# Two-layer mixture-of-experts and attention kernel: the routing chain of the expert passes laid out over other slots

## The chip, the cores and the metric

One core of a Trainium2 chip runs the whole program in one launch. The metric is the device time of one execution in microseconds, the median of several runs.

## The reference

The input x is 4 x 1024 tokens of 128 numbers, float32. Six blocks are added to it in turn, each fed by a layer normalisation of x where the code says so. Four of them are expert blocks, and only these are touched:

```python
x = x + 0.5 * _L0_ffn_ref(_layernorm(x), ...)   # ffn0a
x = x + _L0_attn_ref(_layernorm(x), ...)
x = x + 0.5 * _L0_ffn_ref(_layernorm(x), ...)   # ffn0b
x = x + 0.5 * _L1_ffn_ref(_layernorm(x), ...)   # ffn1a
x = x + _L1_attn_ref(_layernorm(x), ...)
x = x + 0.5 * _L1_ffn_ref(_layernorm(x), ...)   # ffn1b
```

A layer-0 expert block has 16 experts of 64 hidden numbers in 4 groups, and a shared one. The router's sigmoid scores plus a bias pick the best 2 groups by their best expert, then the best 4 experts of these; the sigmoid scores are the weights. A layer-1 block has 8 experts of 256 hidden numbers; the best 2 logits are taken, and their softmax over these two are the weights (the kernel writes it as 0.5 + 0.5 tanh of half the difference from their mean sum). Both compute silu(x W1) * (x W3) for every expert, times its weight, and project back to 128 numbers.

## The kernel before, in words

All experts are computed for all tokens, and the weight of an expert that was not picked is zero. `phase_moe` (called four times from `build`) does one expert pass. It goes over the 4096 tokens in 8 groups of 512, and within a group over chunks of 128 hidden numbers: NC is 9 in layer 0 and 16 in layer 1. Every engine runs the same two loops, written out when the program is built, `for h in range(g0 - 2, end)` over groups and `for c in range(NC)` over chunks. One turn of the inner loop is called a slot here. Each engine executes its own list strictly in order and waits on semaphores.

One chunk passes five engines' hands. To keep float32 accuracy each operand is a sum of a high and a low part in the rounded format fp32r, so each product is three matmuls of 512 columns:

- TensorE, `up_and_gate` (L319, L322): three matmuls for gate, three for up, into one of three PSUM banks each.
- ScalarE, `silu` (L401): silu of the gate bank. Then, in the same slot, `high` of the chunk before (L406): the high part of the hidden product.
- VectorE, `scale` (L553): times the expert weights, a row copied over all lanes (the tile `share`); `hide` (L563): times up. In layer 0 the ninth chunk is the shared expert and has no scale.
- GpSimd, `low` (L438): hidden product minus its high part.
- TensorE, `project` (L331 to L333): three matmuls, two slots later (LAG = 2), which wait for low.

Beside the chunks of group h run the preparation steps of the next groups and the last steps of the one before. The dict `slot` says in which slot each stands, and `chain` calls it there, after the chunk's own work on that engine. Steps named in `early` are done for group h + 2, the others for h + 1; yout, yturn and y (the output's evacuation, transposition and addition to x) are for h - 1. The steps in their order:

- stats, aggr (VectorE, L459, L467 to L471): mean and variance; rstd (GpSimd, `invert`, L432 and L434): a power and a product; norm (ScalarE, L371): x normalised, four tiles of 128 x 128 in one go.
- turn (TensorE, L292): four transposes into the PSUM bank `misc`; xh (ScalarE, L377) and xl (VectorE, L475): its high and low part.
- logit (TensorE, L298 to L300), lout (ScalarE, L381), lturn (TensorE, L305): router logits, tokens on lanes.
- r1 to r4 (VectorE, L495 to L540, with ScalarE's tanh at L386 or L391): a chain of small steps of which each waits for the one before (`step`): scores, the 8 largest (L488), marks by match_replace of four tiles (L511, L532), the penalty of groups not kept (L513), the combine weights `comb` (L540). ROUTE is the count of these steps.
- cturn (TensorE, L311): comb transposed; ScalarE copies it to `combt` (L395); SyncE writes it to memory (L266) and copies it back over the lanes as `share` (L273), 16 copies in layer 0 and 8 in layer 1.

All transposes, the logits and y share the one bank `misc`, so their order on TensorE is fixed, and turn waits for comb_t, yturn (L348) for a step of the next group's routing. Memsets of the tile `unread` (L78) stand between some of the small VectorE steps.

In ffn0b and ffn1a the weights of the next phase are loaded in pieces and split (`ahead`, class SplitAhead: L1116 on SyncE, L1124 on ScalarE, L1129 on GpSimd), two pieces a group, in slots 1 and NC // 2 by `piece_at`.

Of the kernel before, what the change touches and what calls it, by code (L numbers as in the profile page):

```python
# [9 lines left out]
ALU = mybir.AluOpType  # L10
# [154 lines left out]
def phase_moe(nc, k, tag, layer, turn_no, ahead=None, out=None):  # L165
# [17 lines left out]
    if first:  # L183
        slot = dict(stats=7, aggr=7, rstd=8, norm=8, turn=0, xh=0, xl=0, logit=2, lout=2, lturn=3,
                    r1=3, r2=4, r3=5, r4=5, cturn=6, yout=2, yturn=4, y=4)
    else:
        slot = dict(stats=13, aggr=13, rstd=14, norm=14, turn=1, xh=1, xl=1, logit=3, lout=3, lturn=5,
                    r1=5, r2=7, r3=9, r4=10, cturn=11, yout=2, yturn=7, y=8)
    early = ("stats", "aggr", "rstd", "norm")
# [18 lines left out]
    def piece_at(g, c):  # L208
        n = 2 * (g - g0 - 1) + (0 if c == 1 else 1)
        return n if ahead is not None and g > g0 and c in (1, NC // 2) and n < ahead.count else None  # L210

    with ExitStack() as ctx:
# [74 lines left out]
        def _(pe):  # L287
# [20 lines left out]
            def cturn(g):  # L308
                pe.wait_ge(route, (g + 1) * ROUTE)
                for t in range(TG):  # L310
                    mm = pe.transpose(misc[0:NE, t * P:(t + 1) * P], comb[:, t, :], k.ident)  # L311
                mm.then_inc(comb_turned, 1)
# [54 lines left out]
        def _(act):  # L367
            def norm(g):
                act.wait_ge(rstd_done, 2 * g + 2)
                for t in range(TG):  # L370
# [42 lines left out]
            for h in range(g0 - 2, end):  # L413
                for c in range(NC):
# [8 lines left out]
                    chain(h, c, (("norm", norm), ("xh", xh), ("lout", lout), ("r1", r1), ("r2", r2), ("cturn", cturn)))  # L423
# [30 lines left out]
        def _(dve):  # L454
# [49 lines left out]

            def r2(g):
                if first:
                    step(top(gext, top_sb), g)
                    step(dve.memset(top_sb[:, :, 2:8], PAD), g)
                    pause(dve, k)
                    for t in range(TG):  # L510
                        ins = dve.match_replace(gmark[:, t, :], top_sb[:, t, :], gext[:, t, :], TAKEN)  # L511
                    step(ins, g)
                    step(dve.tensor_scalar(pen[:].rearrange("p (e t) -> p e t", t=TG),  # L513
                                           gmark[:, :, 0:5].rearrange("p t e -> p e t"), TAKEN, OUT, ALU.not_equal,
                                           ALU.mult), g)
# [5 lines left out]
            def r3(g):  # L521
                if first:
                    wide = pen[:, 0:4 * TG].rearrange("p (e t) -> p t e", t=TG).unsqueeze(3).broadcast_to([P, TG, 4, 4])
# [4 lines left out]
                else:  # L528
                    step(dve.memset(top_sb[:, :, 2:8], PAD), g)
                pause(dve, k)  # L530
                for t in range(TG):
# [1107 lines left out]
```

## Time and profile before

| | us |
|---|---|
| median of 3 runs | 2052.0 (2049.13 to 2074.68) |
| the profiled execution | 2051.49 |
| its span, first to last instruction | 2049.7 |
| mean granted clock of TensorE | 0.924 of full |
| TensorE matmuls busy | 1723.2 (84%) |
| VectorE busy | 1351.5 (66%) |
| ScalarE busy | 1004.0 (49%) |
| GpSimd busy | 736.8 (36%) |

The profile is of one execution, and its instruction records give start and length of each. PE is TensorE's matmuls, PEld its weight loads, DVE VectorE, ACT ScalarE, POOL GpSimd, SPq SyncE's queue. Busy matmuls overlap in the records: they are pipelined. From the first gate matmul of one group to that of the next, the expert passes take the time that the first section of rows below divides by seven. The first gate matmul of ffn0a starts at 34.11 us, that of ffn0b at 912.28, of ffn1a at 1163.58 and of ffn1b at 1715.79.

### The profile page before, as it was taken

How to read it: one execution, taken by the hardware profiler on the slowest of the kernel's cores; microseconds unless marked ns; L12 is line 12 of the kernel's file. 1: busy time of each engine (PE TensorE's matmuls, PEld its weight loads, DVE VectorE, ACT ScalarE, POOL GpSimd, SP SyncE). 2: the span in 40 equal slices, each digit the busy share in tenths (PEclk: the TensorE clock that was granted, in tenths of full speed). 3: DMA queues.
4: the chain of work that ended last, by engine and by line, in shares of the span. 5: the costliest groups of instructions: out<-in, count | busy, mean ns of one | idle time of the engine just before them, and what ended most of it. 6: DMA issues, size and time to landing. Idle time of an engine off the chain costs nothing. (4 is left out here: it accounts for less than half of the span.)

```text
span 2049.7 us, 26334 instructions
## 1 busy us (share of the span) xinstructions
PE 1723.2 (84%) x8440; PEld 1206.2 (59%) x8440; DVE 1351.5 (66%) x4086; ACT 1004.0 (49%) x1687; POOL 736.8 (36%) x693
## 2 busy tenths in 40 slices
PE   3888869899899899968888699989967775989998
PEld 2666645545555555436666477767755664767776
DVE  4676658778778778536656466666667765666665
ACT  3555415555555565644554355455532223555554
POOL 3444411311312211114544355555520102555555
PEclk9999959999999999979888899999988897999999
DMA  4222211111110110003232211211100001121111
GB/s 130 84 78 69 64 28 30 18 24 28 18 34 18 21 31 18 10 25 103 78 104 74 95 42 42 75 50 42 42 1 0 0 0 42 51 84 47 47 52 52
DMA packets 58086, 94.98 MB, mean 46 GB/s; under 512 B 9297, under 2 KB 16850, under 8 KB 57954
## 3 DMA queue, kind: packets, MB, share of 16 engines
q1 hardware_dynamic: 55842, 91.08, 15.9%
q10 hardware_dynamic: 2112, 2.30, 0.4%
q8 instruction: 64, 1.05, 0.2%
q14 instruction: 68, 0.56, 0.1%
HBM read 76.76 MB, written 2.88 MB: 39 GB/s over the span
## 5 line engine op out<-in xcount | busy, mean ns | idle before, releaser
L909 ACT ACTIVATE att_probs<-banks 128x1024 f32<-128x1024 f32 (+3 forms) x384 | 306.1, 812 | 194.1 <-PE banks L820 192.0
L401 ACT ACTIVATE banks<-banks 128x512 f32<-128x512 f32 x384 | 223.3, 582 | 246.3 <-PE banks L319 239.9
L1034 DVE CUSTOM_DVE_ANT_0 banks<-banks,att_mask 128x128 f32<-128x128 f32 (+3 forms) x512 | 234.4, 525 | 70.6 <-PE banks L801 70.1
L801 PE MATMUL banks<-arena 128*128 128x512 f32 (+3 forms) x768 | 249.1, 406 | 27.9 <-DMA arena<-att_parts 15.3
L949 POOL TENSOR_SCALAR_AFFINE_SELECT att_probs<-att_probs 128x512 f32<-128x512 f32 x128 | 81.6, 637 | 419.7 <-ACT att_probs L909 419.7
L801 PEld LDWEIGHTS banks<-arena 128*128 128x128 f32 x768 | 132.7, 197 | 150.5 <-issue 90.8
L438 POOL TENSOR_TENSOR ffn1a_hid_l<-ffn1a_hid,ffn1a_hid_h 128x512 fp32r<-128x512 f32 x128 | 165.6, 1294 | 153.0 <-ACT ffn1a_hid_h L406 153.0
L438 POOL TENSOR_TENSOR ffn1b_hid_l<-ffn1b_hid,ffn1b_hid_h 128x512 fp32r<-128x512 f32 x128 | 165.3, 1292 | 152.1 <-ACT ffn1b_hid_h L406 152.1
L820 PE MATMUL banks<-arena 128*128 128x512 f32 (+3 forms) x768 | 204.4, 351 | 0.5 <-ACT att_probs L909 0.4
L1036 DVE TENSOR_REDUCE att_mx<-banks 128x1 f32<-128x512 f32 x256 | 162.2, 684 | 32.0 <-PE banks L801 31.8
L839 PE MATMUL banks<-att_probs,att_v_aug 128*32 128x512 f32 (+3 forms) x1536 | 166.4, 505 | 0.6 <-POOL att_probs L949 0.5
L553 DVE TENSOR_TENSOR ffn1a_scl<-banks,ffn1a_share 128x512 f32<-128x512 f32 x128 | 88.4, 691 | 103.5 <-ACT banks L401 92.8
L553 DVE TENSOR_TENSOR ffn1b_scl<-banks,ffn1b_share 128x512 f32<-128x512 f32 x128 | 88.4, 691 | 103.1 <-ACT banks L401 92.5
L820 PEld LDWEIGHTS banks<-arena 128*128 128x128 f32 x768 | 137.3, 190 | 26.0 <-ACT att_probs L909 11.3
L438 POOL TENSOR_TENSOR ffn0b_hid_l<-ffn0b_hid,ffn0b_hid_h 128x512 fp32r<-128x512 f32 x72 | 92.4, 1284 | 116.3 <-ACT ffn0b_hid_h L406 116.3
L438 POOL TENSOR_TENSOR ffn0a_hid_l<-ffn0a_hid,ffn0a_hid_h 128x512 fp32r<-128x512 f32 x72 | 92.5, 1286 | 112.5 <-ACT ffn0a_hid_h L406 112.4
L319 PE MATMUL banks<-ffn1a_xh,arena 128*128 128x512 f32 x256 | 106.7, 417 | 0.0
L319 PE MATMUL banks<-ffn1b_xh,arena 128*128 128x512 f32 x256 | 106.6, 416 | 0.0
L322 PE MATMUL banks<-ffn1a_xh,arena 128*128 128x512 f32 x256 | 103.5, 404 | 0.0
L322 PE MATMUL banks<-ffn1b_xh,arena 128*128 128x512 f32 x256 | 103.3, 404 | 0.0
L563 DVE TENSOR_TENSOR ffn1b_hid<-ffn1b_scl,banks 128x512 f32<-128x512 f32 x128 | 88.0, 687 | 4.4
L563 DVE TENSOR_TENSOR ffn1a_hid<-ffn1a_scl,banks 128x512 f32<-128x512 f32 x128 | 88.0, 687 | 4.4
(390 smaller groups left out, 3890.8 us busy)
## 6 DMA issues: line engine op xcount, KB each, us to landing
ffn0a_share<-weight_rows SPq DMA_DIRECT2D x128, 128.0 KB, 3.0
ffn0b_share<-weight_rows SPq DMA_DIRECT2D x128, 128.0 KB, 3.0
ffn1a_share<-weight_rows SPq DMA_DIRECT2D x64, 256.0 KB, 4.3
ffn1b_share<-weight_rows SPq DMA_DIRECT2D x64, 256.0 KB, 4.5
arena<-att_parts SPq DMA_DIRECT2D x16, 384.0 KB
arena<-att_parts SPq DMA_DIRECT2D x128, 48.0 KB
w_raw<-in_ffn_w_dram SPq DMA_DIRECT2D x12, 256.0 KB, 3.2
out_dram<-x SPq DMA_DIRECT2D x8, 256.0 KB, 2.3
```

The costliest lines, as they stand in the source:

```text
L319: mm = pe.matmul(gate_ps[:, num % NB, :], w[:, ws], xx[:, g % 2, :], start=m == 0, stop=m == 2)
L322: mm = pe.matmul(up_ps[:, num % NB, :], w[:, ws], xx[:, g % 2, :], start=m == 0, stop=m == 2)
L401: act.activation(gate if c < NSCALED else sil[:], gate, ACT.Silu).then_inc(silu_done, 1)
L438: pool.tensor_tensor(hid_l[:, num % NH, :], hid[:, num % NH, :], hid_h[:, num % NH, :].bitcast(F32), ALU.subtract).then_inc(low_cut, 1)
L553: dve.tensor_tensor(scl[:, num % 2, :], gate_ps[:, num % NB, :], share[:, c // PER, :], ALU.mult)\
L563: dve.tensor_tensor(hid[:, num % NH, :], scl[:, num % 2, :] if c < NSCALED else sil[:], up_ps[:, num % NB, :], ALU.mult).then_inc(hidden, 1)
L801: mm = pe.matmul(bank[:, at:at + width], q_st[:, n % 3, t * P:(t + 1) * P], k_pad[:, n % 2, j, c * G:c * G + width], start=True, stop=True ...
L820: mm = pe.matmul(score_ps[:, pair, h, 0:c], k_pad[:, n % 2, 2 * pair + h, kb * P:(kb + 1) * P], q_st[:, n % 3, (qg + 1) * G - c:(qg + 1) * ...
L839: mm = pe.matmul(o_ps[32 * j:32 * j + 32, G - c:G], v_aug[:, b % 2, kb, at:at + 32], probs[:, unit % NPROB, j, 0:c], start=kb == 0, stop=k ...
L909: act.activation(probs[:, unit % NPROB, 2 * pair:2 * pair + 2, 0:c], score_ps[:, pair, :, 0:c], ACT.Exp, scale=SCALE).then_inc(exped, 1)
L1034: ins = dve.tensor_tensor_reduce(now, now, mask[:, G - width:G], 1.0, -3e38, ALU.add, ALU.max, best)
L1036: ins = dve.tensor_reduce(best, now, AX.X, ALU.max)
```

## The change

The same work is done with the same instructions. The dict `slot` is new in both layers; norm is cut into two halves of two tiles each (norm and norm2) that stand in slots of their own; the marking by match_replace is one function `taken`, and the routing chain has five parts instead of four. In layer 0 the whole path up to xl is done for group h + 2 (early), with turn, xh and xl in slot 8. The transposition of comb has a further wait, for the addition of y of the group two before (y_added). The pieces of weights loaded ahead are split in slots 3 and 6 (layer 0) or 5 and 10 (layer 1).

```diff
--- before.py
+++ after.py
@@ -181,12 +181,14 @@
     ROUTE = 12 if first else 8
 
     if first:
-        slot = dict(stats=7, aggr=7, rstd=8, norm=8, turn=0, xh=0, xl=0, logit=2, lout=2, lturn=3,
-                    r1=3, r2=4, r3=5, r4=5, cturn=6, yout=2, yturn=4, y=4)
+        slot = dict(stats=0, aggr=1, rstd=1, norm=3, norm2=4, turn=8, xh=8, xl=8, logit=1, lout=1, lturn=2, r1=2, r2=2,
+                    r3=3, r4=4, r5=5, cturn=7, yout=2, yturn=5, y=6)
+        early = ("stats", "aggr", "rstd", "norm", "norm2", "turn", "xh", "xl")
     else:
-        slot = dict(stats=13, aggr=13, rstd=14, norm=14, turn=1, xh=1, xl=1, logit=3, lout=3, lturn=5,
-                    r1=5, r2=7, r3=9, r4=10, cturn=11, yout=2, yturn=7, y=8)
-    early = ("stats", "aggr", "rstd", "norm")
+        slot = dict(stats=11, aggr=12, rstd=12, norm=14, norm2=15, turn=1, xh=1, xl=1, logit=3, lout=3, lturn=4, r1=4,
+                    r2=5, r3=7, r4=8, r5=8, cturn=10, yout=2, yturn=6, y=7)
+        early = ("stats", "aggr", "rstd", "norm", "norm2")
+    PIECES = (3, 6) if first else (5, 10)
 
     def rows(g):
         return slice((g - g0) * G, (g - g0 + 1) * G)
@@ -206,8 +208,8 @@
                 f(g)
 
     def piece_at(g, c):
-        n = 2 * (g - g0 - 1) + (0 if c == 1 else 1)
-        return n if ahead is not None and g > g0 and c in (1, NC // 2) and n < ahead.count else None
+        n = 2 * (g - g0 - 1) + (0 if c == PIECES[0] else 1)
+        return n if ahead is not None and g > g0 and c in PIECES and n < ahead.count else None
 
     with ExitStack() as ctx:
         def sem(name):
@@ -307,6 +309,7 @@
 
             def cturn(g):
                 pe.wait_ge(route, (g + 1) * ROUTE)
+                at_least(pe, y_added, g - 1)
                 for t in range(TG):
                     mm = pe.transpose(misc[0:NE, t * P:(t + 1) * P], comb[:, t, :], k.ident)
                 mm.then_inc(comb_turned, 1)
@@ -367,7 +370,12 @@
         def _(act):
             def norm(g):
                 act.wait_ge(rstd_done, 2 * g + 2)
-                for t in range(TG):
+                for t in range(TG // 2):
+                    act.activation(xn[:, t, :], k.x[:, tile_of(g, t)], ACT.Identity, bias=nshift[:, t:t + 1],
+                                   scale=rstd[:, t:t + 1])
+
+            def norm2(g):
+                for t in range(TG // 2, TG):
                     ins = act.activation(xn[:, t, :], k.x[:, tile_of(g, t)], ACT.Identity, bias=nshift[:, t:t + 1],
                                          scale=rstd[:, t:t + 1])
                 ins.then_inc(norm_done, 1)
@@ -420,7 +428,7 @@
                             high(h * NC + c - 1)
                         if piece_at(h, c) is not None:
                             ahead.high(act, piece_at(h, c))
-                    chain(h, c, (("norm", norm), ("xh", xh), ("lout", lout), ("r1", r1), ("r2", r2), ("cturn", cturn)))
+                    chain(h, c, (("norm", norm), ("norm2", norm2), ("xh", xh), ("lout", lout), ("r1", r1), ("r2", r2), ("cturn", cturn)))
             high(end * NC - 1)
             yout(end - 1)
 
@@ -502,23 +510,32 @@
                     step(dve.tensor_copy(ext[:, :, 0:NE], misc3[:, :, 0:NE]), g)
                     step(top(ext, top_sb), g)
 
+            def taken(rest, dst):
+                pause(dve, k)
+                for t in range(TG):
+                    ins = dve.match_replace(dst[:, t, :], top_sb[:, t, :], rest[:, t, :], TAKEN)
+                return ins
+
             def r2(g):
                 if first:
                     step(top(gext, top_sb), g)
                     step(dve.memset(top_sb[:, :, 2:8], PAD), g)
-                    pause(dve, k)
-                    for t in range(TG):
-                        ins = dve.match_replace(gmark[:, t, :], top_sb[:, t, :], gext[:, t, :], TAKEN)
-                    step(ins, g)
+                else:
+                    step(dve.tensor_tensor(hs[:], top_sb[:, :, 0:1], top_sb[:, :, 1:2], ALU.add), g)
+                    step(dve.scalar_tensor_tensor(df[:], hs[:].broadcast_to([P, TG, E1]), -0.5, ext[:, :, 0:NE],
+                                                  ALU.mult, ALU.add), g)
+
+            def r3(g):
+                if first:
+                    step(taken(gext, gmark), g)
                     step(dve.tensor_scalar(pen[:].rearrange("p (e t) -> p e t", t=TG),
                                            gmark[:, :, 0:5].rearrange("p t e -> p e t"), TAKEN, OUT, ALU.not_equal,
                                            ALU.mult), g)
                 else:
-                    step(dve.tensor_tensor(hs[:], top_sb[:, :, 0:1], top_sb[:, :, 1:2], ALU.add), g)
-                    step(dve.scalar_tensor_tensor(df[:], hs[:].broadcast_to([P, TG, E1]), -0.5, ext[:, :, 0:NE],
-                                                  ALU.mult, ALU.add), g)
-
-            def r3(g):
+                    step(dve.memset(top_sb[:, :, 2:8], PAD), g)
+                    step(taken(ext, mark), g)
+
+            def r4(g):
                 if first:
                     wide = pen[:, 0:4 * TG].rearrange("p (e t) -> p t e", t=TG).unsqueeze(3).broadcast_to([P, TG, 4, 4])
                     ext4 = ext[:, :, 0:NE].rearrange("p t (g e) -> p t g e", e=4)
@@ -526,16 +543,12 @@
                     step(top(ext, top_sb), g)
                     step(dve.memset(top_sb[:, :, 4:8], PAD), g)
                 else:
-                    step(dve.memset(top_sb[:, :, 2:8], PAD), g)
-                pause(dve, k)
-                for t in range(TG):
-                    ins = dve.match_replace(mark[:, t, :], top_sb[:, t, :], ext[:, t, :], TAKEN)
-                step(ins, g)
-                if not first:
                     dve.wait_ge(tanh_done, g + 1)
                     step(dve.tensor_scalar(sig[:], th[:], 0.5, 0.5, ALU.mult, ALU.add), g)
 
-            def r4(g):
+            def r5(g):
+                if first:
+                    step(taken(ext, mark), g)
                 at_least(dve, comb_turned, g)
                 step(dve.scalar_tensor_tensor(comb[:], mark[:, :, 0:NE], TAKEN, sig[:], ALU.is_equal, ALU.mult), g)
                 assert count[0] == ROUTE, count[0]
@@ -574,7 +587,7 @@
                             scale(h, c)
                         hide(h, c)
                     chain(h, c, (("stats", stats), ("aggr", aggr), ("xl", xl), ("r1", r1), ("r2", r2), ("r3", r3),
-                                 ("r4", r4)))
+                                 ("r4", r4), ("r5", r5)))
             add(end - 1)
 
 
```

## Rows read from the trace of the kernel before

**Rows 1.** Windows, seven groups each: PE, PEld, DVE, ACT, POOL, clock, DMA, GB/s.

```profile
34.11:226.91 192.80, 157.69 (x692) 120.35 (x690) 131.50 (x459) 100.75 (x189) 86.84 (x75) 0.97 0.25 79
912.28:1123.05 210.77, 179.89 (x692) 136.17 (x690) 127.20 (x459) 106.72 (x201) 100.71 (x87) 0.83 0.29 89
1163.58:1457.72 294.14, 271.33 (x1133) 207.25 (x1132) 187.86 (x451) 153.19 (x289) 153.70 (x127) 0.94 0.18 57
1715.79:2005.58 289.79, 267.72 (x1132) 204.04 (x1131) 187.43 (x451) 151.86 (x286) 150.31 (x124) 0.96 0.20 62
```

**Rows 2.** Waits in ffn0a, ffn0b, ffn1a, ffn1a: total, times, longest (us).

```profile
PE banks L292 <- ACT ffn0a_xn L371: 14.0, 7, 2.1
...
PE banks L311 <- DVE ffn0b_comb L540: 13.0, 7, 1.9
...
PE banks L331 <- POOL ffn1a_hid_l L438: 21.7, 9, 3.3
...
ACT ffn1a_th L391 <- DVE ffn1a_df L518: 11.5, 7, 1.7
```

**Rows 3.** Timeline of ffn0b, TensorE's matmuls: start us, us, engine, line.

```profile
1046.64 0.39 PE L333 MATMUL banks<-ffn0b_hid_l,wdh 128*128 128x512 f32 x1
1046.87 0.60 PE L348 MATMUL banks<-pack,ffn0b_y_t 128*128 128x128 f32 x4
...
1047.54 0.39 PE L319 MATMUL banks<-ffn0b_xl,wgh 128*128 128x512 f32 x1
...
1055.80 0.63 PE L319 MATMUL banks<-ffn0b_xl,wgh 128*128 128x512 f32 x1
1056.22 0.63 PE L319 MATMUL banks<-ffn0b_xh,wgl 128*128 128x512 f32 x1
```

**Rows 4.** Timeline of ffn1a, one chunk from scale to low.

```profile
1391.54 0.69 DVE L553 TENSOR_TENSOR ffn1a_scl<-banks,ffn1a_share 128x512 f32<-128x512 f32 x1 [0.66 <-ACT banks L401]
1392.27 0.69 DVE L563 TENSOR_TENSOR ffn1a_hid<-ffn1a_scl,banks 128x512 f32<-128x512 f32 x1
...
1393.54 0.58 ACT L401 ACTIVATE banks<-banks 128x512 f32<-128x512 f32 x1 [1.50 <-PE banks L319]
1394.04 0.62 ACT L406 ACTIVATE ffn1a_hid_h<-ffn1a_hid 128x512 fp32r<-128x512 f32 x1
...
1394.74 1.30 POOL L438 TENSOR_TENSOR ffn1a_hid_l<-ffn1a_hid,ffn1a_hid_h 128x512 fp32r<-128x512 f32 x1 [1.33 <-ACT ffn1a_hid_h L406]
```

**Rows 5.** Timeline of ffn1a, the norm path of one group.

```profile
1412.84 0.16 DVE L471 TENSOR_SCALAR ffn1a_veps<-ffn1a_mv 128x4 f32<-128x4 f32 x1
...
1414.12 1.00 POOL L432 TENSOR_TENSOR ffn1a_rstd<-ffn1a_veps,neghalf 128x4 f32<-128x4 f32 x1
...
1415.44 1.65 ACT L371 ACTIVATE ffn1a_xn<-x,ffn1a_nshift,ffn1a_rstd 128x128 f32<-128x128 f32 x4 [2.65 <-POOL ffn1a_nshift L434]
```

**Rows 6.** Timeline: routing of ffn0b; steps beside low in ffn1a, ffn0a.

```profile
1052.33 0.22 DVE L525 TENSOR_TENSOR ffn0b_ext<-ffn0b_ext,ffn0b_pen 128x64 f32<-128x64 f32 x1
...
1053.21 0.09 DVE L532 MATCH_VALUE_LOAD ffn0b_mark<-ffn0b_top,ffn0b_ext 128x8 f32 x1
...
1053.94 0.55 DVE L540 SCALAR_TENSOR_TENSOR ffn0b_comb<-ffn0b_mark,ffn0b_sig 128x64 f32<-128x64 f32 x1
...
1397.55 0.56 DVE L517 TENSOR_TENSOR ffn1a_hs<-ffn1a_top 128x4 f32<-128x4 f32 x1
...
1396.80 1.29 POOL L438 TENSOR_TENSOR ffn1a_hid_l<-ffn1a_hid,ffn1a_hid_h 128x512 fp32r<-128x512 f32 x1 [0.76 <-ACT ffn1a_hid_h L406]
...
172.59 1.28 DVE L470 TENSOR_SCALAR ffn0a_nmean<-ffn0a_mv 128x4 f32<-128x4 f32 x1
```

**Rows 7.** Timeline of ffn0a, the first weights from ScalarE to the first scale.

```profile
34.57 0.59 ACT L395 ACTIVATE ffn0a_combt<-banks 16x512 f32<-16x512 f32 x1 [5.23 <-PE banks L311]
...
36.79 5.63 SPq L273 DMA_DIRECT2D ffn0a_share<-weight_rows  x9
...
40.32 0.69 DVE L553 TENSOR_TENSOR ffn0a_scl<-banks,ffn0a_share 128x512 f32<-128x512 f32 x1 [5.27 <-DMA ffn0a_share<-weight_rows]
```

More of the change, by code:

```diff
@@ L508, in r2 @@
                     step(dve.memset(top_sb[:, :, 2:8], PAD), g)
-                    pause(dve, k)
-                    for t in range(TG):
-                        ins = dve.match_replace(gmark[:, t, :], top_sb[:, t, :], gext[:, t, :], TAKEN)
-                    step(ins, g)
-                    step(dve.tensor_scalar(pen[:].rearrange("p (e t) -> p e t", t=TG),
-                                           gmark[:, :, 0:5].rearrange("p t e -> p e t"), TAKEN, OUT, ALU.not_equal,
-                                           ALU.mult), g)
                 else:
@@ L521, in r3 @@
             def r3(g):
+                if first:
+                    step(taken(gext, gmark), g)
+                    step(dve.tensor_scalar(pen[:].rearrange("p (e t) -> p e t", t=TG),
+                                           gmark[:, :, 0:5].rearrange("p t e -> p e t"), TAKEN, OUT, ALU.not_equal,
+                                           ALU.mult), g)
+                else:
+                    step(dve.memset(top_sb[:, :, 2:8], PAD), g)
+                    step(taken(ext, mark), g)
+            def r4(g):
                 if first:
```

## Prediction, made before the changed kernel ran

> **What bounds the kernel now.** I read the four expert passes alone: the change touches nothing else. A pass is 8 groups; I call one turn of the inner loop over c a slot (9 in the ffn0 passes, 16 in ffn1). The table by windows, from the first gate matmul of group 1 to that of group 8, gives seven whole groups of each pass: 192.80, 210.77, 294.14 and 289.79 us, so 27.5, 30.1, 42.0 and 41.4 us a group [rows 1].
>
> What would TensorE alone need? In its timeline one matmul of 512 columns starts 0.23 us after another (1046.64, then 1046.87) at the full clock, 0.2275 over a long run; four transposes and the matmul behind them take 1046.87 to 1047.54, so the transposes add 0.44 [rows 3]. A slot has 9 matmuls, 2.05 us; a group adds three logit matmuls (0.68) and four sets of transposes (1.76). Bare sums: 20.9 us in ffn0, 35.2 in ffn1. So 6.6, 9.2, 6.8 and 6.2 us a group are stall, 202 us over the 28 groups. No other engine fills a group: VectorE, next in line, is busy 131.50/7 = 18.8 us in ffn0 and 187.86/7 = 26.8 in ffn1 [rows 1]. The time is lost to order, not to load.
>
> Which orders? The waits of TensorE name three. In ffn0a the turn of the normalised input (L292) waits 14.0 us for ScalarE's norm, seven times; in ffn0b the turn of the combine weights (L311) waits 13.0 for VectorE's last routing step, seven times, and each of the two rows has its like in the other pass. In ffn1 one line is left, the down projection (L331) waiting for GpSimd's low half, 21.7 us in ffn1a (3.1 a group, up to 3.3 at once) and as much in ffn1b [rows 2]. The third kind of loss is the clock: after such stops matmuls stand 0.42 us apart instead of 0.23, its lower level (1.2 GHz) [rows 3]; the granted clock is 0.83 in ffn0b against 0.97 in ffn0a, and TensorE's busy time is 22.2 us more for the same matmuls [rows 1].
>
> How little a chunk can bear is seen in one chunk of ffn1a: scale at 1391.54, hide 1392.27 to 1392.96, but high only at 1394.04, since ScalarE does the next chunk's silu first (1393.54), and low 1394.74 to 1396.04 [rows 4]; the projection waits for that. This chunk's next slot has transposes (0.44); without them high stands some 0.55 to 0.65 us behind hide's end. So VectorE may be about 0.55 us late, ScalarE and GpSimd may not be late at all.
>
> **The change, part by part.**
>
> *Norm path of ffn1.* Now: statistics and aggregate in slot 13, then GpSimd's pow and shift, during which ScalarE stands in front of norm: veps 1412.84, rstd 1414.12, norm 1415.44 for 1.65 us [rows 5]; silu and high of two slots come behind it. This is the 3.1 us stop of slot 0, and the clock behind it: a mean of 0.94 [rows 1] is 12% of 42 us, 5 us, at the lower level, of which up to half is lost. I put both at 4.6 us a group. After: norm is two slots behind pow, split into two times 0.85 us in slots 14 and 15. Silu and high hold ScalarE for 1.1 us (1393.54 to the end of high) of a slot of 2.05 [rows 4], so a half just fits: 0. What is late next: GpSimd. It takes pow and shift (1414.12 to 1415.44, 1.3 us) in slot 12, the very slot of the aggregate, and meets veps only about 3.6 us after that slot's first matmul (0.95 to the gate, silu, scale and hide 2.0, aggregate 0.65), half a microsecond before low of chunk 12 is due (high's end, 4.1): that low starts 0.7 us late, and there is no slack behind it. Cost 0.7.
>
> *Routing of ffn1.* r1 to slot 4: a copy and a top of four tiles, at most the 0.88 us of ffn0's mask add and top (1052.33 to 1053.21) [rows 6], beside VectorE's 0.7 idle in a slot and 0.55 slack: 0. r2 alone in slot 5: ScalarE's tanh stands in front of silu 6 until VectorE has df; today it waits 11.5/7 = 1.65 us [rows 2], of which 0.95 would be idle: 0.7; in a slot without transposes 0.8. Marking in slot 7 with add (0.8 + 0.6 against 1.25): under 0.1. Sigma and comb in slot 8: 0.1. cturn in slot 10, with comb two slots old: no wait; its new wait for y_added has the add of slot 7 behind it, done six microseconds before: 0, and only the next gate matmuls stand behind it. Of today's 6.8, after 4.6 and 0.7, 1.5 is left, small waits at slots with transposes and where xh and yout share ScalarE; I keep 1.3. Sum 35.2 + 0.7 + 0.8 + 0.2 + 1.3 = 38.2 us. Bounds: 36 (everything but the tanh hidden) and 40 (half of today's stall).
>
> *Norm path of ffn0.* Statistics, aggregate and pow in slots 0 and 1, norm in 3 and 4, turn and split in slot 8: the turn wait (2 us a group) and the norm block go, since xn is four slots old. Pow in slot 1 meets low 1 as above, here with VectorE also late by the statistics: 1.0 us.
>
> *Routing of ffn0.* Now mask add, top, mark and comb fill VectorE from 1052.33 to 1054.49 in one piece [rows 6], and L311 waits. After, the mask add and top (0.88) are in slot 4, mark and comb (0.73 + 0.6) in slot 5, the first mark and pen (0.9) in slot 3, and cturn comes two slots after comb: the wait goes. Of VectorE's 18.8 us, scales and hides are 17 x 0.67 = 11.4, xl and add 1.3, the norm path 1.5; 4.6 is routing, so r1 and r2 together in slot 2 are 1.5. Against 0.7 idle (1.15 with transposes) slots 2 to 5 run 0.8 us behind in sum, 0.55 of it borne. Followed from chunk 0, with one step blocked as below, TensorE waits 0.4 us in projections 3 to 6.
>
> *The weights' way back.* It has less time than now. cturn moves from slot 6 to slot 7, and the stop of 3 us between slots 8 and 0 is gone. From combt's start to the first scale that really waited for its share row: 34.57 to 40.32, 5.75 us (16 row copies, 0.63 us of issue each, two of them for the first chunk) [rows 7], plus 0.6 for the transposes before: 6.4. From scale 0 to the end of its low, with nothing in between, 0.73 + 0.73 + 0.6 + 1.3 + gaps = 3.45. From the first projection in slot 2 to cturn of slot 7 TensorE needs 1.1 + 4.1 + 2.5 + 2.05 + 2.05 = 11.8. The ring closes in 21.65 us, 0.75 over the bare sum. SyncE's later rows keep ahead (1.25 us a chunk against 2.05).
>
> Sum ffn0a: ring 21.65 + 1.0 + 0.4 = 23.1. In ffn0b the pieces of the next weights (slots 3 and 6) put 0.62 us on ScalarE beside a norm half, 2.45 us in a 2.05 slot: 0.5 more, 23.6. The clock stays high, since no stop over 1.5 us is left. Bounds: 22 (ring and 0.4) and 26 (three more blocked steps, 3 x 1.29, less 0.9 borne).
>
> *Sum.* Savings a group 4.4, 6.5, 3.8 and 3.2 us, 17.9 by seven groups: 125 us. First and last groups of a pass: 0, since the way to the first cturn keeps all its steps and the last group routes nothing. The profiled execution took 2051.5 us (span 2049.7), the median of the runs is 2052.0; so **1926 us**.
>
> **A rule weighed.** Two steps show VectorE blocked by GpSimd: hs, four numbers a lane, takes 0.56 us from 1397.55 and ends with the low that began at 1396.80 for 1.29; a nmean took 1.28 [rows 6]. The Trainium skill (SBUF — State Buffer, "SBUF: two separate sides") says the pair of ports that VectorE and GpSimd share is an exclusive lock for a whole instruction, taken by two-input or two-port VectorE instructions. By that rule, the trace agrees. It speaks against this change: spreading ten small steps over more slots gives each its own chance of a low in front. It is the second rival.
>
> **Rivals.**
> 1. *Nothing takes the stalls' place* but the ring and tanh: 22.0, 22.3, 36.3, 36.3 a group: saves 5.5, 7.8, 5.7, 5.1, 169 us: 1883. For it: all my late terms are under 1 us. Against: ScalarE and GpSimd have no slack [rows 4].
> 2. *Slower: the blocked steps.* Sig, ext, mask add, pen, comb, nmean, veps, hs each wait for a whole low (1.29), behind each the scale of the next chunk. Today some two a group do. The saving of 4.5 us a group is eaten when 0.65 us passes through at seven steps, and from there it is slower; with all eight blocked for a whole low, less 0.55 borne each, it is 6 us a group over the forecast: 1926 + 168 = 2094. Against: most steps come within 0.7 us of hide's end, before high has let the next low start.
> 3. *The weights' way becomes the bound.* Of the 5.75 us the last copy takes some 2.9 (issued at 37.42, scale at 40.32) and the write ahead of the copies 1.6 (35.2 to 36.79) [rows 7]. Were they 5 and 3 beside the denser work, the ring is 25 us, and 1.4 of pow and chain on top make 26.5: ffn0a saves 1.0, ffn0b 3.1, ffn1 half of its 7.0. 7.6 x 7 = 53: 1999. Seen as VectorE's L553 waiting for DMA in every group.
> 4. *It does not do what it says*: the slots move, but each wait reappears one slot on (turn for comb_t, cturn for y_added), within 2%: 2040.
>
> **How the numbers follow.** Forecast (1926, own range 1900 to 1960) 0.62; rival 1 0.14; rival 3 0.17; rival 4 0.05; rival 2 0.02. Two per cent, about what a measurement can tell, is 41 us. The range 1880 to 1990 takes in rival 1 and most of rival 3. Faster by over 2%: 0.62 + 0.14 + 0.16 = 0.92; within: 0.05 + 0.01 = 0.06; slower: 0.02.
>
> **What would show it.** TensorE's waits at L292 and L311 gone inside a pass; groups of 23, 23.5, 38, 38 us; granted clock of ffn0b at 0.97 or more; new short waits of L331 two slots after pow; in ffn0 a wait of L553 for DMA of about a microsecond at each group's start. I am wrong if that wait is over 3 us, if hs, sig or comb take over 1 us in most groups, or if the clock of ffn0b stays under 0.9.

## The result, and the profile after

Four runs of the changed kernel had a median of 1929.5 us (1926.7 to 1934.7), four of the kernel before 2063.2 (2049.1 to 2074.7): a ratio of 0.936, 95% interval 0.928 to 0.944. Of the kernel before, two runs took 2049 and 2052 us and two 2074; the profiled executions, both in the fast state, took 1929.0 us (span 1927.3) and 2051.5 (2049.7), which is 0.940. The forecast was 1926 us.

Windows of the changed kernel over the same seven groups of each pass; columns as in [rows 1]:

```profile
35.76:196.96 161.20, 154.39 (x688) 116.95 (x688) 125.12 (x450) 98.83 (x184) 85.79 (x73) 1.00 0.29 94
886.75:1049.24 162.49, 154.15 (x688) 116.56 (x687) 125.36 (x450) 104.77 (x196) 99.94 (x85) 0.99 0.36 113
1092.37:1359.86 267.49, 258.65 (x1133) 198.11 (x1132) 187.78 (x451) 153.04 (x289) 153.78 (x127) 0.99 0.20 65
1618.68:1883.94 265.26, 259.58 (x1133) 197.91 (x1131) 186.18 (x451) 151.62 (x286) 150.33 (x124) 0.99 0.22 70
```

Divided by seven, groups take 23.0, 23.2, 38.2 and 37.9 us, where [rows 1] had 27.5, 30.1, 42.0 and 41.4. Over the bare sums of 20.9 and 35.2 that leaves 2.1, 2.3, 3.0 and 2.7 us, 71 us in all, of the 202 before. ScalarE and GpSimd are busy as long as before. TensorE's busy time fell by 25.7 us in ffn0b for the same matmuls, with the granted clock at 0.99 and no longer 0.83.

Waits of the changed kernel in the windows of ffn0a, ffn1a and ffn1b (total, times, longest, in us):

```profile
DVE ffn0a_scl L566 <- DMA ffn0a_share<-weight_rows: 13.7, 7, 2.7
...
PE banks L334 <- POOL ffn0a_hid_l L446: 6.7, 14, 0.9
...
ACT ffn1a_th L399 <- DVE ffn1a_df L525: 12.3, 7, 2.2
...
PE banks L334 <- POOL ffn1a_hid_l L446: 8.0, 10, 3.4
...
PE banks L334 <- POOL ffn1b_hid_l L446: 4.8, 8, 2.1
```

The two transposition waits of [rows 2] have no like here: in these windows TensorE no longer stops at the turn (now L294) or at the transposition of the combine weights (L314). Its wait for low in ffn1a fell from 21.7 to 8.0 us. One wait is new: in each ffn0 group a scale waits 13.7/7 = 2.0 us on average for its weights' DMA (before, only that of group 1 did). ScalarE's tanh waits as before (12.3 against 11.5).

One group of ffn0a in the changed kernel, timeline, rows of VectorE, TensorE and GpSimd (start us, us; in brackets the idle time before and what ended it):

```profile
125.87 0.60 PE L314 MATMUL banks<-pack,ffn0a_comb 128*16 128x128 f32 x4
...
132.36 0.69 DVE L566 TENSOR_TENSOR ffn0a_scl<-banks,ffn0a_share 128x512 f32<-128x512 f32 x1 [1.86 <-DMA ffn0a_share<-weight_rows]
...
135.95 0.47 PE L334 MATMUL banks<-ffn0a_hid_h,wdh 128*128 128x512 f32 x1 [0.53 <-POOL ffn0a_hid_l L446]
...
137.76 1.29 POOL L446 TENSOR_TENSOR ffn0a_hid_l<-ffn0a_hid,ffn0a_hid_h 128x512 fp32r<-128x512 f32 x1
...
137.90 1.24 DVE L504 TENSOR_TENSOR ffn0a_ext<-ffn0a_sig,gate_bias 128x64 f32<-128x64 f32 x1
...
149.29 0.60 PE L314 MATMUL banks<-pack,ffn0a_comb 128*16 128x128 f32 x4
```

These rows hold the weights' ring: from cturn to the first scale 6.5 us, to the first projection 3.6 more, to the next cturn 13.3; 23.4 in this group. And they show a blocked step: ext, 64 numbers a lane, started 0.14 us after a low and ended 0.1 us after it, 1.24 us for what takes 0.22 to 0.23 elsewhere. It is so in six of the eight groups of both ffn0 passes.

One slot of ffn1a where GpSimd's pow stands ahead of low:

```profile
1167.41 1.01 POOL L440 TENSOR_TENSOR ffn1a_rstd<-ffn1a_veps,neghalf 128x4 f32<-128x4 f32 x1 [0.22 <-DVE ffn1a_veps L479]
...
1168.65 1.28 POOL L446 TENSOR_TENSOR ffn1a_hid_l<-ffn1a_hid,ffn1a_hid_h 128x512 fp32r<-128x512 f32 x1
...
1169.99 0.50 PE L334 MATMUL banks<-ffn1a_hid_h,arena 128*128 128x512 f32 x1 [0.39 <-POOL ffn1a_hid_l L446]
```

The low stands right behind pow and shift, and the projection two slots later waits 0.39 us for it, as the prediction had it for slot 14.

*Where 8.7 us were given back.* The seven groups of all passes saved 31.6 + 48.3 + 26.7 + 24.5 = 131.1 us, the span only 122.4. Timelines of both kernels put it at the ends of the passes (us, before and after). Here and below a group or slot is read from the weight load of its first gate matmul, which starts up to 0.2 us ahead of the matmul; this is also what the 34.11 us and the windows of [rows 1] are (the matmul itself starts at 34.18).

| | ffn0a | ffn0b | ffn1a | ffn1b |
|---|---|---|---|---|
| first statistics to first gate | 15.6, 17.5 | 15.6, 17.5 | 13.7, 13.6 | 13.6, 13.6 |
| group 1 | 26.1, 23.8 | 26.1, 23.6 | 41.3, 41.8 | 41.4, 40.3 |
| groups 2 to 7, mean | 27.8, 22.9 | 30.8, 23.1 | 42.1, 37.6 | 41.4, 37.5 |
| group 8, gate 1 to gate of its last chunk | 18.2, 19.4 | 18.5, 21.2 | 32.3, 32.4 | 32.3, 32.4 |

Group 1 gains hardly anything in any pass: with the way to the gate added it is 41.7 us before and 41.2 after in ffn0a. The timelines of VectorE say why: from the first statistics to the first scale, which waits for the first weights, it is 21.8 us before and 22.0 after in ffn0a, 21.8 and 21.9 in ffn0b, 19.6 and 19.7 in ffn1a, 19.4 and 19.4 in ffn1b. In ffn1 group 1 also scatters: ffn1b's takes 40.3, 40.3, 42.0 and 42.2 us in the changed kernel, e6, e5 and e11 (experiments of the next section), which are alike there, so single values of this line are good to about 2 us. Groups 2 to 7 gain more than the mean, 4.9, 7.6, 4.5 and 3.9 us. Group 8 of the ffn0 passes lost 1.2 and 2.6 us; its first scale waits 3.8 and 3.9 us for its weights. The attention between ffn0a and ffn0b took 1.4 us more.

### The profile page after: what moved, and what is told of

The parts are those of the page before. It is cut to its first block and busy times, and to the rows that moved or that the text cites. A ratio compares the mean times of both kernels' runs of the same rounds, so it can differ in the third digit from the quotient of the medians.

```text
span 1927.3 us, 26366 instructions
## 1 busy us (share of the span) xinstructions
PE 1678.1 (87%) x8440; PEld 1171.3 (61%) x8440; DVE 1343.7 (70%) x4086; ACT 1004.0 (52%) x1687; POOL 737.5 (38%) x693
## 5 line engine op out<-in xcount | busy, mean ns | idle before, releaser
L322 PE MATMUL banks<-ffn1a_xh,arena 128*128 128x512 f32 x256 | 103.9, 406 | 0.0
L325 PE MATMUL banks<-ffn1a_xh,arena 128*128 128x512 f32 x256 | 101.0, 394 | 0.0
```

The costliest lines, as they stand in the source:

```text
L322: mm = pe.matmul(gate_ps[:, num % NB, :], w[:, ws], xx[:, g % 2, :], start=m == 0, stop=m == 2)
L325: mm = pe.matmul(up_ps[:, num % NB, :], w[:, ws], xx[:, g % 2, :], start=m == 0, stop=m == 2)
```

## The experiments

Each edit is given against the changed kernel unless another is named, and only the entries that differ. Each was timed beside the kernel before, on four chips (e1 to e4, e5 to e8, e9 and e10, e11), where the kernel before had medians of 2051.5 to 2058.7 us; so a difference of a few microseconds between kernels of different chips rests on the group times, not on the medians.

**One half of the change alone.** In the first, the routing and the pieces stand where they stood before, and only the norm path is new; in the second it is the other way round.

```diff
 # e1_norm_only: ffn0, ffn1, pieces
-logit=1, lout=1, lturn=2, r1=2, r2=2, r3=3, r4=4, r5=5, cturn=7, yturn=5, y=6
+logit=2, lout=2, lturn=3, r1=3, r2=4, r3=4, r4=5, r5=5, cturn=6, yturn=4, y=4
-lturn=4, r1=4, r2=5, r3=7, r4=8, r5=8, cturn=10, yturn=6, y=7
+lturn=5, r1=5, r2=7, r3=9, r4=9, r5=10, cturn=11, yturn=7, y=8
-PIECES = (3, 6) if first else (5, 10)
+PIECES = (1, 4) if first else (1, 8)
```

```diff
 # e2_routing_only: ffn0 (turn, xh, xl for group h + 1 again), ffn1, pieces
-stats=0, aggr=1, rstd=1, norm=3, norm2=4, turn=8, xh=8, xl=8
+stats=7, aggr=7, rstd=8, norm=8, norm2=8, turn=0, xh=0, xl=0
-stats=11, aggr=12, rstd=12, norm=14, norm2=15
+stats=13, aggr=13, rstd=14, norm=14, norm2=14
-PIECES = (3, 6) if first else (5, 10)
+PIECES = (1, 4) if first else (1, 8)
```

> The norm path of the change alone (statistics to xl, halves of norm), with the routing slots and the weight pieces of before. Theory (each stop is separate): in ffn0 the wait at the turn goes and the one at cturn stays, 25 and 25.7 us a group; in ffn1 the stop of slot 0 and the low clock behind it go, 38.2. Saves 2.5 + 4.4 + 3.8 + 3.2 = 13.9 us a group column, times 7 = 97: about 1955 us. Rival (either stop left keeps TensorE's clock low and the group long in ffn0): ffn0b stays at 28 or more and its granted clock under 0.9, total 1975 or more.

> The routing slots of the change alone (five parts, cturn two slots behind comb), with norm path and pieces of before. Theory: in ffn0 only the wait at cturn (1.9 us, and the late projection before it) goes, 24.7 and 26 us a group; ffn1 gains under 0.3. Saves about (2.8 + 4.1 + 0.2 + 0.2) x 7 = 51: about 2000 us, and with the norm path alone the two add up to the whole change within 20 us. Rival (VectorE's order was the limit everywhere): ffn1 gains over 1 us a group too, 1985 or less.

Measured: the norm path alone 1967.8 us (ratio 0.957, 0.950 to 0.964), the routing alone 2007.4 (0.978, 0.971 to 0.985). The product, 0.936, is the ratio of the whole change, though the move of the pieces (e6: 6 us) is in neither half. By groups, ffn0a, ffn0b, ffn1a, ffn1b, the norm path saves 1.5, 4.0, 4.1 and 3.3 us, the routing 2.6, 4.2, -0.2 and -0.5, the whole 4.5, 6.9, 3.8 and 3.5. The norm path alone lies between its theory (1955) and its rival (1975 or more); its clock in ffn0 is 0.93 and 0.94, neither under 0.9 nor back at 0.99. The routing alone is 7 us over its theory. What each leaves is the other's wait. The norm path alone, waits in ffn0a:

```profile
PEld banks L312 <- DVE ffn0a_comb L551: 16.1, 7, 2.4
```

The routing alone, waits in ffn1a:

```profile
ACT ffn1a_xn L372 <- POOL ffn1a_nshift L440: 18.2, 7, 2.8
...
PE banks L332 <- POOL ffn1a_hid_l L444: 22.1, 9, 3.1
```

So in ffn1 all of the gain is the norm path's: groups 2 to 7 take 37.5 us in both passes with it alone, and 37.6 and 37.5 in the changed kernel. The -0.2 and -0.5 of the routing alone have a further cause in them: there veps takes 1.0 us on average in ffn1, for 0.16 before, and pow waits for it. In ffn0 both halves are needed. With the norm path alone cturn waits 2.3 us a group for comb.

**The halves of norm.**

```diff
 # e3_norm_whole
-norm=3, norm2=4
+norm=3, norm2=3
-norm=14, norm2=15
+norm=14, norm2=14
```

> The changed kernel with norm in one go again (slot 3 in ffn0, slot 14 in ffn1). Theory: ScalarE then has 1.65 + 1.1 us in a slot of 2.05 and no slack behind it, so the next silu and high are 0.7 us late: 0.6 us a group in all 28, about +17 us, 1946. Rival (the distance to pow was what mattered, the halves are worth nothing): 1929 within 4 us, since in ffn1 the late low of pow already makes the stop of slot 14.

Measured: 1933.4 us (1930.9 to 1940.4), groups 23.3, 23.3, 38.2, 37.9. Whole or in halves it is the same within 4 us: the 1946 expected did not come, the rival held.

**Pow away from low.** Where veps comes just before low is due, pow and shift delay it. In the next kernel pow has a slot of its own behind the aggregate in ffn0, and in ffn1 the statistics stand in slots 2 and 3, and pow in 4.

```diff
 # e4_pow_placed: ffn0, ffn1
-stats=0, aggr=1, rstd=1
+stats=0, aggr=1, rstd=2
-stats=11, aggr=12, rstd=12
+stats=2, aggr=3, rstd=4
 # e7_pow_placed_norm_whole: as e4, and norm2=3 / norm2=14
```

> The changed kernel with GpSimd's power and shift one slot behind the aggregate and in slots that have transposes: ffn0 rstd in slot 2; ffn1 stats 2, aggr 3, rstd 4 (norm halves unchanged). Theory (pow meets veps late and pushes the low behind it): the 0.66 us of slot 14 in ffn1 goes, in ffn0 0.5 of the 0.6 in slot 3: (0.6 + 0.6 + 0.5 + 0.5) x 7 = 15 us less, 1914. Rival (1.3 us of pow does not fit GpSimd's idle 0.75 us of a slot, wherever it stands): the wait moves with it, 1925 to 1930.

Measured: 1915.0 us (1911.2 to 1915.7). Slot 14 of ffn1a fell from 2.71 to 2.17 us by the timeline (medians over the groups, as for all slots below), and groups take 22.6, 22.7, 37.7 and 37.7. In ffn0 slot 3 gained 0.66 us, but slot 2 took back 0.3: the weights' way is late there. In ffn0 the edit does more than it says: with low 1 no longer late, ext is blocked in no group:

```profile
L502 DVE TENSOR_TENSOR ffn0a_ext<-ffn0a_sig,gate_bias 128x64 f32<-128x64 f32 x7 | 1.6, 226 | 0.2
```

In the changed kernel this mean is 1090 ns. How the 0.45 us a group that ffn0 gains divides between the low and the block of ext is not shown; in ffn1 no such step changed.

> The kernel with pow placed in slots 2 (ffn0) and 4 (ffn1), and norm in one go in slots 3 and 14. In the changed kernel the halves were worth 0.1 us a group, because pow's late low made the stop of slot 14 already. Theory (ScalarE has 1.65 + 1.1 us in a slot of 2.05): with that stop gone the whole norm shows, 0.6 us in each of the 28 groups, the slot of projection 13 in ffn1 (slot 15 or 14) at 2.7 us: 1915 + 15 = 1930. Rival (halves never matter, high of one chunk may be late): 1915 within 4.

Measured: 1927.2 us (1925.1 to 1932.5), 12 us more than e4; the next slot 0 of ffn1 grew from 2.17 to 2.56 us. So the halves are worth 12 us, but only with pow placed. In ffn1 the stop at slot 14 had hidden the whole norm: in e3 slot 14 takes 2.75 us and the next slot 0 2.18, in e7 they take 2.17 and 2.56.

**cturn one slot earlier.**

```diff
 # e5_cturn6: ffn0
-cturn=7
+cturn=6
 # e8_pow_placed_cturn6: as e4, and cturn=6 in ffn0
```

> The changed kernel with cturn of ffn0 one slot behind comb (slot 6) instead of two. Theory (the ring of the weights' way back is what holds projection 0 in slot 2, 0.9 us a group): the rows land 2 us earlier, slot 2 falls from 3.4 to 2.5 us, comb is just ready at the end of slot 6, so cturn waits 0.2 to 0.4; ffn0 groups 22.3 to 22.5, 0.7 x 14 = 10 us less, 1919. VectorE's scale waits for the DMA 0.3 us a group at most instead of 2.0. Rival (a step has to stand two slots behind its producer, as everywhere in the change): cturn waits over 1 us for comb and the group stays at 23 or more, 1929 to 1940.

Measured: 1919.4 us (1918.1 to 1921.4), ffn0 groups 22.7 and 22.7. Slot 2 of ffn0a went from 3.37 to 2.69 us, slot 6 from 1.96 to 3.31: with the shorter ring the first projections come sooner, as the theory had it, but cturn waits 1.0 us for comb, and not the 0.2 to 0.4 expected. Here too ext is blocked in one group of a pass only, for six in the changed kernel, so the 0.3 to 0.6 us a group are not the ring's alone. The last groups of the passes take 17.4 and 17.8 us and no longer 19.4 and 21.2. The changed kernel's last group of ffn0b, timeline of VectorE, says why:

```profile
1053.61 0.69 DVE L566 TENSOR_TENSOR ffn0b_scl<-banks,ffn0b_share 128x512 f32<-128x512 f32 x1 [3.89 <-DMA ffn0b_share<-weight_rows]
```

and the same scale with cturn in slot 6:

```profile
1042.93 0.69 DVE L564 TENSOR_TENSOR ffn0b_scl<-banks,ffn0b_share 128x512 f32<-128x512 f32 x1 [1.54 <-DMA ffn0b_share<-weight_rows]
```

> Both: pow placed (slot 2 and slot 4) and cturn of ffn0 in slot 6. With pow placed, slot 2 of ffn0 grew from 3.4 to 3.8 us, so the ring took back most of what pow gave. Theory (ring binds): here both are gone, ffn0 groups 21.7 to 22.0 instead of 22.6 and 22.7, 0.8 x 14 = 11 us less than 1915: 1904. Rival (cturn's wait for comb binds at 22.5): 1913 to 1916.

Measured: 1910.7 us (1909.9 to 1916.4), groups 22.6, 22.6, 37.8 and 37.6. The 1904 expected were not reached: the two gains in ffn0 don't add, and cturn now waits for comb, as in e5:

```profile
PEld banks L312 <- DVE ffn0a_comb L551: 6.7, 7, 1.0
```

**The pieces where they were.**

```diff
 # e6_pieces_old
-PIECES = (3, 6) if first else (5, 10)
+PIECES = (1, 4) if first else (1, 8)
```

> The changed kernel with the weight pieces split in the slots of before (1 and NC // 2: 1 and 4 in ffn0b, 1 and 8 in ffn1a). Theory: in slot 1 of ffn0b GpSimd then has pow (1.3 us) and a piece (1.3 us) beside a low (1.3) in 2.7 us, so low 1 is late by up to 1.3 more: ffn0b 24.2 us a group for 23.2, 7 us more, 1936; ffn0a, ffn1a and ffn1b as they are. Rival (the move of the pieces does nothing): 1929, ffn0b within 0.2 of 23.2.

Measured: 1935.2 us (1934.8 to 1938.0), ffn0b 24.2 a group and the others as they were. The groups of VectorE's instructions in the ffn0b window (count, busy us, mean ns) show what the pieces do, here with pieces in slots 1 and 4:

```profile
L502 DVE TENSOR_TENSOR ffn0b_ext<-ffn0b_sig,gate_bias 128x64 f32<-128x64 f32 x7 | 7.5, 1079 | 0.2
L540 DVE TENSOR_TENSOR ffn0b_ext<-ffn0b_ext,ffn0b_pen 128x64 f32<-128x64 f32 x7 | 7.4, 1064 | 0.0
...
L476 DVE TENSOR_SCALAR ffn0b_nmean<-ffn0b_mv 128x4 f32<-128x4 f32 x6 | 3.9, 646 | 0.2
```

and in the changed kernel, pieces in slots 3 and 6:

```profile
L504 DVE TENSOR_TENSOR ffn0b_ext<-ffn0b_sig,gate_bias 128x64 f32<-128x64 f32 x7 | 7.6, 1088 | 0.2
...
L542 DVE TENSOR_TENSOR ffn0b_ext<-ffn0b_ext,ffn0b_pen 128x64 f32<-128x64 f32 x7 | 1.9, 267 | 0.0
...
L478 DVE TENSOR_SCALAR ffn0b_nmean<-ffn0b_mv 128x4 f32<-128x4 f32 x6 | 1.0, 170 | 0.2
```

The mask add (L540 in the first, L542 in the second) takes 1.06 us beside a piece and 0.27 without; nmean 0.65 and 0.17. In its own timeline the step at 998.61 takes 1.21 us and ends with a piece's split on GpSimd:

```profile
998.61 1.21 DVE L540 TENSOR_TENSOR ffn0b_ext<-ffn0b_ext,ffn0b_pen 128x64 f32<-128x64 f32 x1
...
998.45 1.29 POOL L1140 TENSOR_TENSOR arena<-w_raw,arena 128x512 fp32r<-128x512 f32 x1
```

This is the block of [rows 6] made and taken away by moving the pieces alone. The two steps take 0.8 + 0.5 us longer, and a group grew by 1.0, but the blocks are not all of its cause. By slots the growth stands in slot 3 (mean 2.53 to 2.90 us), slot 7 (2.72 to 3.35) and slot 8 (2.57 to 2.80), with 0.2 less in slot 2. The part of slot 7 is the mask add's: it holds up the next chunk's hide by 1.0 us and its low by 0.7. The part of slot 3 is mostly what was expected, a piece in front of pow on GpSimd, by which low 1 comes 0.7 us later:

```profile
989.80 1.29 POOL L1140 TENSOR_TENSOR arena<-w_raw,arena 128x512 fp32r<-128x512 f32 x1
991.27 1.01 POOL L438 TENSOR_TENSOR ffn0b_rstd<-ffn0b_veps,neghalf 128x4 f32<-128x4 f32 x1 [0.18 <-DVE ffn0b_veps L477]
```

The piece ends at 991.09, so without any block of nmean pow could have started only 0.1 us sooner.

**VectorE's work ahead of the chain.** From e8 to e9 the statistics and pow of ffn0 go behind comb, and r2 of ffn1 moves to slot 6; from e9 to e10 the turn of ffn1 goes into slot 15 of the group before.

```diff
 # e9_stats_behind_comb: against e8, ffn0 (these three for group h + 3), ffn1
-stats=0, aggr=1, rstd=2
+stats=6, aggr=7, rstd=8
-r2=5
+r2=6
 # e10_turn_early: against e9, ffn1 (turn, xh, xl for group h + 2)
-norm=14, norm2=15, turn=1, xh=1, xl=1
+norm=12, norm2=13, turn=15, xh=15, xl=15
```

> The kernel of e8_pow_placed_cturn6 with one more move: in the ffn0 passes the statistics (stats, aggr, veps on VectorE) and the pow on GpSimd of a group run three groups ahead in slots 6, 7, 8, behind that group's comb, no longer two ahead at the start of the chain; and in the ffn1 passes the half of hid that goes with r2 is put beside it in slot 6. Theory (VectorE's chain from slot 0 to comb sets the length of an ffn0 group): some 1.5 us of VectorE's work leave the chain, the wait of the comb's transpose in slot 6 goes, and an ffn0 group takes 21.7 us instead of 22.55; ffn1 groups go from 37.7 to 37.4. Whole kernel about 1894 us. Rival (VectorE's load as a whole, or ScalarE's order of work, keeps the group at 22.5): 1906 to 1911 us.

Measured: 1911.8 us (1906.5 to 1916.9), the same as e8; groups 22.5, 22.5, 37.6 and 37.7. The theory failed; the time is the rival's, though not by a full VectorE, as its timeline shows. This is VectorE in e9, with the cturn that it lets go:

```profile
132.75 0.69 DVE L565 TENSOR_TENSOR ffn0a_scl<-banks,ffn0a_share 128x512 f32<-128x512 f32 x1 [1.74 <-ACT banks L408]
...
142.66 0.23 DVE L552 SCALAR_TENSOR_TENSOR ffn0a_comb<-ffn0a_mark,ffn0a_sig 128x64 f32<-128x64 f32 x1
142.92 0.69 DVE L557 SCALAR_TENSOR_TENSOR x<-banks,x 128x512 f32<-128x512 f32 x1
...
143.76 0.60 PE L313 MATMUL banks<-pack,ffn0a_comb 128*16 128x128 f32 x4 [0.62 <-DVE x L557]
```

The time won ahead of the chain became idle time (1.74 us), since the chain can't begin before the logits of slot 1 are there. From 132.75 to 143.6 VectorE has hardly a gap, and cturn waits for the last two rows, comb and the addition of y. The length of slots 2 to 6 is thus set by VectorE's work between the logits and comb, the scales and hides among it, and not by its load over the whole group.

> The kernel of e9_stats_behind_comb with the normalisation of the ffn1 passes two slots earlier (12 and 13) and its transposes and both halves of their eviction in slot 15 of the group before, no longer in slots 0 and 1. Theory (the eviction of the transposed rows shares ScalarE with the outputs of the group before, and this makes slots 0 to 3 long): about 4 us less than e9, some 1890 us, slot 3 from 3.1 to 2.7 us. Rival (slot 3 is long because of the logits' own matmuls and eviction): the same time as e9, within 2 us.

Measured: 1905.5 us (1904.0 to 1908.9), ratio to before 0.931 (0.925 to 0.938), the fastest version here. Slot 3 of the ffn1 groups fell from 3.10 to 2.79 us, slots 0 and 1 by 0.2 and 0.5, against 0.55 more in slot 15: a group after the first fell by 0.4 us (in ffn1a from 36.9 to 36.5), and twelve of them make 5 us, where 4 were expected. The times are the theory's; but as xl left VectorE's slot 1 and the transposes TensorE's by the same edit, the sharing of ScalarE as the cause is not shown by itself. By the windows it looks like more, 12.5 us, since group 1 fell by 3.8 in each pass; but its first gate came 3.3 us later, behind the turn:

```profile
1083.42 1.11 PE L293 MATMUL banks<-pack,ffn1a_xn 128*128 128x128 f32 x4 [2.21 <-ACT ffn1a_xn L378]
1084.19 0.77 PE L321 MATMUL banks<-ffn1a_xh,arena 128*128 128x512 f32 x1
```

In e9 the gate came earlier, and the first scale then waited. This is its wait in group 1 of ffn1a; in e10 it is 0.6 us:

```profile
DVE ffn1a_scl L565 <- DMA ffn1a_share<-weight_rows: 6.7, 1, 6.7
```

What group 1 waits for is the arrival of the first weights, behind comb: from the first statistics to that scale it is 19.7 us in e9 and 19.4 in e10, and the 3.3 us put ahead of the gate came back whole.

**The way to the first gate.**

```diff
 # e11_turn_late0: ffn0 (turn, xh, xl for group h + 1 again)
-turn=8, xh=8, xl=8
+turn=0, xh=0, xl=0
```

> The changed kernel with one part undone: in the ffn0 passes turn, xh and xl stand in slot 0 and work for group h + 1 again, so that the input of group 1 is turned behind the first gate matmul of a pass and not ahead of it. Theory (this step is the 1.65 and 1.85 us that the way to the first gate of an ffn0 pass grew by): the first gate of ffn0a starts at 34.1 us, no longer 35.8, and that of ffn0b comes about 1.8 us sooner behind the attention before it; the groups stay at 23.0 to 23.3, the last group at 19.4 and 21.2, and the whole takes about 1926 us. Rival (the first gate was held by something else, a load or the order of the norm halves): it stays at 35.8, and the time at 1929; should the logits in slot 1 wait for the halves of the turned input, groups are 0.3 us longer and the whole takes 1930 to 1934.

Measured: the first gate came at 34.11 us, and 15.6 us behind the first statistics in both ffn0 passes, as in the kernel before, so the turn of group 1 is what had moved it. But nothing was won: group 1 takes 27.0 us in ffn0a (changed: 23.8), and with the way to the gate it is 42.6 against 41.2. The whole took 1945.9 us (1943.8 to 1949.7), which neither theory had. Groups of ffn0 are 24.3 and 24.8 us. In the timeline of its TensorE the cause is:

```profile
114.13 0.40 PE L334 MATMUL banks<-ffn0a_hid_l,wdh 128*128 128x512 f32 x1
116.46 0.50 PE L298 MATMUL banks<-ffn0a_xh,rth 128*128 128x512 f32 x1 [1.93 <-DVE ffn0a_xl L481]
```

and on VectorE:

```profile
113.62 0.69 DVE L564 TENSOR_TENSOR ffn0a_scl<-banks,ffn0a_share 128x512 f32<-128x512 f32 x1 [3.74 <-DMA ffn0a_share<-weight_rows]
...
115.73 0.68 DVE L481 TENSOR_TENSOR ffn0a_xl<-banks,ffn0a_xh 128x512 fp32r<-128x512 f32 x1
```

The scale waits for its weights; behind it on VectorE stand hide and the statistics of slot 0 (0.7 and 0.9 us) and only then the low part xl; and the logits of slot 1 wait for xl, 2.1 us a group. In the kernel before, the statistics stood in slot 7, so part of this wait is their new place and not the turn's. Turning the input a slot ahead saves 1.3 to 1.6 us a group with the statistics in slot 0, and what it puts in front of the first gate comes back in group 1, as in e10.

## Why the prediction was right, step by step

The forecast was 1926 (own range 1900 to 1960), the median 1929.5, by the mechanism that it gave; the savings per group were put at 4.4, 6.5, 3.8 and 3.2 us and are 4.5, 6.9, 3.8 and 3.5. That the total came within 4 us is luck in part: groups 2 to 7 saved 18 us more than forecast, group 1 of the four passes, counted with the way to it, 16 us less, and the last groups of ffn0 lost 3.8.

- *Norm path of ffn1, 4.6 us a group for stop and clock.* Right: the norm path alone saves 4.1 and 3.3 us net of the pow's new price, which e4 puts at 0.5 in ffn1a and 0.2 in ffn1b (slot 14: 0.54) against the 0.7 forecast. TensorE's clock rose to 0.99 and stayed there.
- *"A half just fits: 0."* Right for the halves; but a whole norm in one slot would have cost nothing either, within 4 us (e3), while pow's stop stood next to it. With pow placed, the halves carry 12 us (e7).
- *Routing of ffn1.* Right in sum: forecast was no net gain, measured alone -0.2 and -0.5, and on top of the norm path -0.1 and 0.0 (groups 2 to 7). The tanh cost less than the 0.8 forecast: slot 6 takes 2.73 us, 0.24 over its nine matmuls and transposes, and slot 7 2.36, 0.31 over. With r2 in slot 6 (e9) slot 7 lost 0.41 and slot 8 gained 0.40.
- *Ring, pow and chain in ffn0: 21.65 + 1.0 + 0.4.* The sum is right (23.0 and 23.2 against 23.1), its terms are not. Placing pow (e4), and with it the end of ext's block, takes 0.45 us from a group, not 1.0: its stop of 0.66 in slot 3 had shortened the ring's wait by 0.3. Ring and chain together are then 22.6, where the terms say 22.05. Two legs of the ring read from [rows 7] came out, 6.5 against 6.4 us and 3.6 against 3.45. The third was put at 11.8 and took 13.3 in the group shown, with pow's low and the blocked ext in it. The wait of about a microsecond for the DMA was 2.0.
- *Pieces in ffn0b, +0.5.* Too much: ffn0b is 0.2 us over ffn0a. The prediction looked only at ScalarE's 0.6 us. What the pieces do to GpSimd's pow and to the mask add in their old slots was not seen: with the new routing their move is worth 1.0 us a group (e6), more than ScalarE's part.
- *"First and last groups of a pass: 0."* Wrong. The way to the first cturn keeps all its steps, as the step says, and so the first weights come no sooner (21.8 to 22.0 us behind the first statistics in ffn0, 19.4 to 19.7 in ffn1, before and after). Group 1 waits for them, and its saving, counted in full among the seven, is 0.5, 0.6, -0.5 and 1.1 us with the way to the gate, where 17.9 in all was forecast. Groups 2 to 7 saved more than forecast (4.9, 7.6, 4.5, 3.9) and made up for it. "The last group routes nothing" looked at what that group issues and not at what it needs: its weights come over the same ring, begun a slot later, and its first scale waits 3.8 us in ffn0a and 3.9 in ffn0b. The loss of 3.8 us in both passes is gone in e5. The attention's 1.4 us stay open: from the last gate of ffn0a to the first statistics of ffn0b the profiles of all kernels, with no edit there, lie between 650.3 and 659.1 us.
- *Rival 1* (nothing takes the stalls' place, 1883) did not come; e10 goes half of the way to it from 1926, by removing two of the terms. *Rival 2*, the blocked steps, was a real mechanism, about as large after as before: summed over the small VectorE steps of all passes, the time above each step's shortest was 25.9 us before and is 24.1; ext is now blocked in most ffn0 groups (1.09 us on average in ffn0b), hs of ffn1 in part as before, sig of ffn1 in part now (0.49 us on average, for 0.18) and df of ffn1a (0.39 for 0.19), comb and nmean hardly any more. The Trainium skill (SBUF — State Buffer, "SBUF: two separate sides") names a lock held for a whole instruction, and e6 agrees with it: the mask add of 1.21 us there ends with a GpSimd instruction of 1.29 (998.61 and 998.45, with their lengths 999.8 and 999.7). *Rival 3* would have needed a first wait over 3 us in every group; it is over that only in the last group of each ffn0 pass. *Rival 4* fell: each half alone leaves the other's wait, both together leave none.

## What to carry to other kernels

When an order is moved, follow it at both ends of the loop too: the first turn may be bound by something that the change does not touch, and the last one still needs what now comes later. Remove the larger stop before judging a smaller edit beside it (the halves of norm: no more than 4 us alone, 12 with pow moved). And before work is taken from in front of a chain, ask whether the chain could start earlier at all.

## What the runs showed of the hardware that was not expected

How often a small VectorE step is blocked hangs on where the GpSimd instruction stands, and hardly on the step's size: nmean (128 x 4, a single input from SBUF) takes 0.17 us alone and 0.88 behind a piece's split in four of six groups (e6), where the mask add (128 x 64) takes 1.2 for 0.22. Moving the splits two slots on took two steps from 1.06 and 0.65 us to 0.27 and 0.17. And TensorE's clock, granted at 0.83 in ffn0b when two stops of up to 2 us came in every group, stood at 0.99 there once its longest wait named was 1.4 us. The stops alone don't say how low it goes: with the same two waits it was 0.97 in ffn0a before, and with cturn's alone (e1) it is 0.93 in ffn0a and 0.94 in ffn0b. Why is open.
